# Weighted sums of two attention steps in one burst, with four buffers of exponentials

## The reference

```python
qkv = (x @ Wqkv.T + bqkv).reshape(Bb, Ss, 3, H, HD).transpose(2, 0, 3, 1, 4)
q, k, v = (qkv[0], qkv[1], qkv[2])
attn = jax.nn.softmax(jnp.einsum('bhid,bhjd->bhij', q, k) / jnp.sqrt(jnp.float32(HD)), axis=-1)
...
mod = attn * coh[..., None]
mod = mod / (mod.sum(-1, keepdims=True) + 1e-08)
...
mod = (1.0 - fi) * mod + fi * fa[:, None, :, None]
out = jnp.einsum('bhij,bhjd->bhid', mod, v).transpose(0, 2, 1, 3).reshape(Bb, Ss, Ee)
```

## Time and profile before

| what | value |
|---|---|
| median of 3 runs | 1762.52 us |
| the profiled execution, its time | 1765.92 us |
| its span, first to last instruction | 1764.1 us |
| granted TensorE clock, mean over the span | 0.959 |
| first attention, scores and sums | 116.8 to 485 us |
| TensorE, VectorE, ScalarE busy in 116 to 300 us | 182.03, 155.15, 134.61 us |

### The profile page before, as it was taken

How to read it: one execution, slowest core, us unless ns; L and a number is a source line. 1 busy time by engine, 2 the same in 40 slices (tenths; PEclk the granted TensorE clock), 3 DMA queues, 4 the chain that set the end, 5 groups by cost and what they waited for, 6 DMA issues and landing times. The chain is left out here.

```text
span 1764.1 us, 25261 instructions
## 1 busy us (share of the span) xinstructions
PE 1584.6 (90%) x8692; PEld 1009.6 (57%) x8692; DVE 1159.8 (66%) x1980; ACT 897.0 (51%) x1872; POOL 393.5 (22%) x243
## 2 busy tenths in 40 slices
PE   7789999999968999999978898895999898888698
PEld 3422222222246797878756666663777665665576
DVE  3678888888266464646554953965676873783776
ACT  5137777777813343434325763664434664674442
POOL 3400000000033000000012540553222462262123
PEclk9989999999989999999989999897999999999799
DMA  7621222200003212030033000001002000000010
GB/s 236 125 37 19 37 33 30 30 1 1 1 22 109 72 37 88 19 106 1 0 140 90 1 1 1 0 0 48 1 0 78 1 1 2 0 0 2 23 48 24
DMA packets 59312, 64.74 MB, mean 37 GB/s; under 512 B 15090, under 2 KB 48578, under 8 KB 59220
## 3 DMA queue, kind: packets, MB, share of 16 engines
q1 hardware_dynamic: 57860, 60.24, 13.3%
q10 hardware_dynamic: 1360, 3.41, 0.5%
HBM read 52.95 MB, written 10.49 MB: 36 GB/s over the span
## 5 line engine op out<-in xcount | busy, mean ns | idle before, releaser
L576 DVE TENSOR_REDUCE mcol<-bank 128x1 f32<-128x1024 f32 x256 | 301.4, 1218 | 55.7 <-PE bank L567 55.7
L661 ACT ACTIVATE a_pt<-bank 128x512 f32<-128x512 f32 x512 | 266.3, 602 | 88.4 <-PE bank L693 88.3
L693 PE MATMUL bank<-qa,ka 99*128 99x512 bf16 x512 | 193.0, 384 | 7.2 <-ACT a_pt L661 3.8
L567 PE MATMUL bank<-ka,qa 96*128 96x512 bf16 x512 | 192.7, 386 | 7.4 <-DVE mcol L576 4.2
L1854 PE MATMUL bank<-m_hn,m_w 128*128 128x512 f32 x576 | 151.2, 419 | 18.9 <-DVE m_hn L1985 16.4
L1397 PE MATMUL bank<-wqkv,w_hst 128*128 128x512 f32 x576 | 142.8, 411 | 17.4 <-DVE w_hst L1604 17.4
L1368 POOL TENSOR_TENSOR w_sm<-w_sm,w_st 128x1024 f32<-128x1024 f32 (+1 forms) x64 | 132.3, 2078 | 88.8 <-DVE w_st L1645 88.8
L1854 PEld LDWEIGHTS bank<-m_hn,m_w 128*128 128x128 f32 x576 | 112.2, 195 | 56.2 <-issue 27.3
L693 PEld LDWEIGHTS bank<-qa,ka 99*128 99x128 bf16 x512 | 49.0, 98 | 165.3 <-ACT a_pt L661 120.7
L1443 PE MATMUL bank<-w_kT,w_qz 128*128 128x256 f32 (+1 forms) x512 | 127.3, 385 | 17.9 <-DVE w_st L1638 7.9
L1397 PEld LDWEIGHTS bank<-wqkv,w_hst 128*128 128x128 f32 x576 | 113.2, 197 | 48.1 <-DVE w_hst L1604 20.3
(11 more groups left out here) (237 smaller groups left out, 2673.5 us busy)
## 6 DMA issues: line engine op xcount, KB each, us to landing
f_wex<-in_W SPq DMA_DIRECT2D x8, 2048.0 KB, 11.7
qa<-q_parts SPq DMA_DIRECT2D x48, 128.0 KB, 4.5
ka<-k_parts SPq DMA_DIRECT2D x48, 128.0 KB, 5.3
q_parts<-p_parts SPq DMA_DIRECT2D x16, 192.0 KB, 3.0
k_parts<-p_parts SPq DMA_DIRECT2D x8, 384.0 KB, 3.3
wqkv_raw<-in_wqkv SPq DMA_DIRECT2D x2, 1536.0 KB, 8.8
w<-in_w SPq DMA_DIRECT2D x2, 1536.0 KB, 7.7
phi<-in_phi SPq DMA_DIRECT2D x5, 512.0 KB, 3.7
```

Of the source, the lines that this page charges most:

```text
L567: last = nc.tensor.matmul(max_bank(G, r)[:, jh * HALF:(jh + 1) * HALF], G["qa"][k][0:KS, hg % 2, h, it * P:(it + 1) * P], G["ka"][k][0:KS, ...
L576: nc.vector.reduce_max(G["mcol"][hg % 2][:, p:p + 1], max_bank(G, r)[:, :], X).then_inc(G["max_free"], 1)
L661: nc.scalar.activation(pt[n % 2][:, q, :], sbank(HG * step + q), ACT.Exp, scale=HD0 ** -0.5).then_inc(p_ready, 1)
L693: mm(sbank(i), ka[k][:, q, n * P:(n + 1) * P], qa[k][:, ih, q, :], start=True, stop=True).then_inc(st_ps, 1)
```

## The change

Two things. `pt` has four buffers instead of two, and ScalarE waits for the sums of four steps ago. And `weighted` is called only in even steps, for the two steps before, one right behind the other; in the odd steps none stands, so that the scores and maxima of an odd step and the next even one follow each other without sums between them. The copy of `obank` moves from behind the exponentials of step 0 to behind those of step 1, and the last two steps' sums stand at the end. Banks of scores and of maxima are as before.

```diff
--- before.py
+++ after.py
@@ -623,7 +623,7 @@
         sb = lambda n, s, dt=F32: ctx.enter_context(nc.sbuf_tensor(n, s, dt))
         sem = lambda n: ctx.enter_context(nc.semaphore(n))
         PB, qa, ka, vst, OT = G["PB"], G["qa"], G["ka"], G["vst"], G["OT"]
-        pt = [sb(f"a_pt{s}", [P, HG, HALF]) for s in range(2)]
+        pt = [sb(f"a_pt{s}", [P, HG, HALF]) for s in range(4)]
         st_ps, p_ready, pv_done, o_out = sem("a_st_ps"), sem("a_p_ready"), sem("a_pv_done"), sem("a_o_out")
         sbanks = (PB[0][:, 0:HALF], PB[0][:, HALF:T], PB[1][:, 0:HALF])
         sbank = lambda i: sbanks[i % 3]
@@ -654,13 +654,13 @@
                 for hg in range(HALVES):
                     for n in range(TT):
                         step = TT * hg + n
-                        if step >= 2:
-                            act.wait_ge(pv_done, step - 1)
+                        if step >= 4:
+                            act.wait_ge(pv_done, step - 3)
                         for q in range(HG):
                             act.wait_ge(st_ps, HG * step + q + 1)
-                            nc.scalar.activation(pt[n % 2][:, q, :], sbank(HG * step + q), ACT.Exp,
+                            nc.scalar.activation(pt[n % 4][:, q, :], sbank(HG * step + q), ACT.Exp,
                                                  scale=HD0 ** -0.5).then_inc(p_ready, 1)
-                        if n == 0 and hg >= 1:
+                        if n == 1 and hg >= 1:
                             act.wait_ge(pv_done, TT * hg)
                             nc.scalar.activation(OT[:, (hg - 1) // 2, (hg - 1) % 2 * HALF:((hg - 1) % 2 + 1) * HALF], obank,
                                                  ACT.Copy).then_inc(o_out, 1)
@@ -702,7 +702,7 @@
                     pe.wait_ge(p_ready, HG * (step + 1))
                     for q in range(HG):
                         last = mm(obank[32 * q:32 * q + 32, :], vst[hg // 2 % 2][:, jt, q, :],
-                                  pt[jt % 2][:, q, :], start=(jt == 0), stop=(jt == TT - 1))
+                                  pt[jt % 4][:, q, :], start=(jt == 0), stop=(jt == TT - 1))
                     last.then_inc(pv_done, 1)
 
                 pe.wait_ge(G["ones_in"], GB + 2)
@@ -717,8 +717,10 @@
                                 maxima_to_rows(nc, pe, G, hg + 1)
                             if ahead < HALVES:
                                 score_pair(nc, pe, G, ahead, p0 + q // 2, (q % 2,))
-                        if hg + n > 0:
+                        if n % 2 == 0 and hg + n > 0:
+                            weighted(TT * hg + n - 2)
                             weighted(TT * hg + n - 1)
+                weighted(TT * HALVES - 2)
                 weighted(TT * HALVES - 1)
```

## The result

The changed kernel takes 1788.35 us (median of 4 runs, 1786.33 to 1792.39) against 1762.57 us for the kernel before (1761.11 to 1764.72): a ratio of 1.0148, 95% interval [1.0127, 1.0169]. That is 25.8 us slower, 22 to 30 by the interval. I had predicted 1792 us, 29.1 slower.

What follows compares the result with a forecast made beforehand. The prediction took TensorE to set the pace in the first attention stage, VectorE and ScalarE following with some slack. Terms of 17.6, 8.3, 0.3 and 2.9 us made 29.1, on 1762.5: 1792 us, range 1782 to 1806.

Steps and rivals of the forecast that it cites:

- The burst's saving: Weighted sums of two steps together: the second step costs TensorE 0.86 us instead of 1.09, saving 0.23 us a pair.
- the rival with the dearer step: The second step of a burst costs 1.09 us instead of 0.86: 15 us more, 1806 us; chance 0.08.
- The two banks of maxima: Four pairs of maxima in a row wait 0.39 and 0.26 us for VectorE's reductions: two steps take 6.12 instead of 5.70 us.
- The sign: After the change, TensorE's maxima matmuls (L567) wait for VectorE's reductions (L576) 100 to 115 times, 30 to 40 us in all.
- The cycle with the transpose: Once per half, the maxima are transposed and VectorE starts reducing later: 0.59 us more for that cycle, 14 times.
- The tail: The last 12 steps, without maxima, where scores wait for exponentials: 2.9 us more in all, 1.65 of it from five cycles.
- the copy: ScalarE's copy of the sums (L665) in the tail, between exponentials that scores wait for: about 0.4 us more.
- the 0.86 us for the last sums: At the very end, step 126's sums no longer lie beside step 127's exponentials: one more step of sums, 0.86 us.
- The sum: Ordinary cycles 17.6, those with transposed maxima 8.3, the first cycle 0.3, the tail 2.9: 29.1 us slower.
- a gain: Rival: VectorE frees its banks in time and the waits fall away: 4 us faster, 1758.5 us; chance 0.04.
- The clock: Rival: TensorE's clock falls in the waits, for a tenth of the stage: 20 us more, 1812 us; chance 0.04.

Runs made afterwards that it cites:

- the half exponentials: The changed kernel with each exponential taken of 256 of 512 columns, reductions whole: 1789.29 us in a single run, stage 391.3 us against 396.1.
- the reordering: The changed kernel with the sixteen score and maxima matmuls between two bursts in another order: 1.0107 of the time before, stage 387.2 us.
- before_half_reduce: The kernel before, with VectorE's reductions reading 512 of 1024 columns: 0.9975 of the time before, stage 369.3 us.
- step5_order: The kernel before, with scores moved ahead of maxima in step 5, which holds the transpose: 0.9980 of the time before, stage 365.0 us.
- after_half_reduce: The changed kernel with VectorE's half reductions, reading 512 of 1024 columns: 0.9964 of the time before, stage 366.6 us.
- before_half_both: The kernel before, with reductions reading 512 of 1024 columns and exponentials 256 of 512 (both cuts): 0.9973 of the time before, stage 364.8 us.
- after_half_both: The changed kernel, with reductions reading 512 of 1024 columns and exponentials 256 of 512 (both cuts): 0.9902 of the time before, stage 351.4 us.
- bursts_but_in_tail: The changed kernel, but with single sums from step 5 of half 14 on: 1.0173 of the time before, stage 396.7 us.
- burst_of_four: The changed kernel with sums of four steps together every fourth step and eight exponential buffers: 1.0222 of the time before, stage 405.2 us.

## Why the prediction was right, step by step

- **The burst's saving**, 0.23 us in a pair from the earlier trace rows: 0.24 in an ordinary cycle by the pair of kernels with both cuts. In the changed kernel's trace a double burst takes 1.86 us up to the next score (180.05 to 181.91), as worked out. The cheaper second step of the expert matmuls carried over, and the rival with the dearer step is out.
- **The two banks of maxima**, the step on which all hung: right in place and size. Ordinary cycle 6.11 us (predicted 6.12), 42 of them at 0.42. Read from the starts, the third pair comes 0.47 us late and the fourth 0.17, together 0.64 of the 0.65 predicted. Shown by the half reductions (the loss goes), the half exponentials (it stays), the reordering (it shrinks as priced). The sign "some 100 to 115 times, for 30 to 40 us" came out with 109 times and, by starts, 38 us (27 in the ordinary cycles, 11 in those with the transpose). The profile's own sums are not that number: 68.2 us counts idle weight loads, 16.0 idle matmuls.
- **The cycle with the transpose**: 6.70 us against 6.13 before, 0.57 (predicted 0.59), but for a wrong reason. I wrote that TensorE loses 0.43 us to the transpose in both kernels. The transpose costs 0.12 us of TensorE (182.13 to 182.25 after). In before the other 0.31 is the wait for the reduction of the step before. A second wait, for VectorE's split, lies behind it and costs nothing more: the matmul that it holds starts at 156.70, 0.22 behind its neighbour.

```profile
155.81 0.10 PEld L567 LDWEIGHTS bank<-ka,qa 96*128 96x128 bf16 x1 [0.54 <-DVE mcol L576]
...
156.48 0.38 PE L693 MATMUL bank<-qa,ka 99*128 99x512 bf16 x1
...
156.67 0.10 PEld L567 LDWEIGHTS bank<-ka,qa 96*128 96x128 bf16 x1 [0.31 <-DVE mrow L597]
156.70 0.38 PE L567 MATMUL bank<-ka,qa 96*128 96x512 bf16 x1
```

After, the first is gone (the burst in front gives VectorE time) and the second now costs 0.30, with its matmul at 183.42 instead of 183.12:

```profile
182.13 0.27 PE L582 MATMUL bank<-ident,mcol 128*16 128x128 f32 x1
182.14 0.10 PEld L567 LDWEIGHTS bank<-ka,qa 96*128 96x128 bf16 x1
182.25 0.38 PE L567 MATMUL bank<-ka,qa 96*128 96x512 bf16 x1
...
183.41 0.10 PEld L567 LDWEIGHTS bank<-ka,qa 96*128 96x128 bf16 x1 [0.63 <-DVE mrow L597]
```

  The two kernels lose the same time there only because the split lets TensorE go on 1.50 us behind the step's first score in both, at 156.67 and 183.41. before_half_reduce shows that either wait is enough: without the first, step 5 still takes 3.26 us against 3.28. step5_order confirms it: what is a wait can be filled.
- **The tail**: 2.2 us (it takes 30.53 us after, 28.37 before) where I had 2.9. Five cycles at 0.36 and the copy at 0.36 once more make 2.2, against my 1.65 and 0.4; the term that failed is the 0.86 us for the last sums. Behind the last scores TensorE's order is the same in both kernels, the sums of step 126 and then those of 127, so there was nothing to lose. From the first score of step 127 to the end it takes 3.67 us in both. The sums of step 126 wait only for their own exponentials and lie beside those of step 127; only the second half of the burst waits, 0.99 us. The first row is of before, the next two of after:

```profile
482.88 2.21 PE L704 MATMUL bank<-a_pt,vst 128*32 128x512 f32 x16
```

```profile
509.98 2.21 PE L704 MATMUL bank<-a_pt,vst 128*32 128x512 f32 x16
...
511.12 0.16 PEld L704 LDWEIGHTS bank<-a_pt,vst 128*32 128x32 f32 x8 [0.99 <-ACT a_pt L661]
```

  I had given that burst one wait, for all its exponentials, where it has two, one for each step.
- **The sum**: 17.4 for the ordinary cycles, 8.0 for those with the transpose, 0.3 at the start, 2.2 in the tail: 27.9, and the stage grew by 27.8. Predicted 29.1. The forecast is right because its largest term is; the tail's error of 0.7 and the misread transpose hardly touch the sum.
- **The rivals**: a gain needed shorter reductions. With 0.69 us instead of 1.22 (after_half_reduce) it came, 2.7 us under its base (4 in the prediction); how short they must be was not tried. The clock didn't fall in the cycles' waits of 0.4 us (0.99 and 1.00 in both stretches).

The Trainium skill ("TensorEngine Tiling (Array Packing)", Key Properties) says that a change of tiling mode drains the engine. The traces agree with the 0.24 us saved in an ordinary cycle, in which one burst's entry and exit fall away; that it is a drain which costs this time, no run shows by itself. The same page of the Trainium skill, "PSUM Bottleneck", says that the copying out of PSUM may become the bottleneck. The trace agrees, with the banks of the maxima, which no tiled matmul fills: VectorE's reading of them cost 0.64 us of waits in a cycle, against the 0.24 saved.

## What to carry to other kernels

Before work on the busiest engine is gathered into longer bursts, count how many results the stretch between bursts then hands to each other engine, and compare with the buffers: with two banks the third result waits for the first to be read, however idle the reader is on average. VectorE was busy 84% of the time and had slack in every step; the slack was of use only while the burst came after every second pair. And read the waits of the step that looks dear before giving its price to the instruction in it: here the transpose took 0.12 us and the wait for a bank behind it 0.31.

## What the runs showed of the hardware

- Matmuls on 32-column strips follow each other at an even pace: 16 of them take 1.92 us and 32 take 3.64 (fp32, 512 columns), so that a further step is 0.86 us. Entering and leaving such a burst costs 0.24 us together, by before_half_both (5.69 us for two steps) and after_half_both (5.45).
- In the tail of bursts_but_in_tail a wait of TensorE of 1.6 us was followed by the lower clock level: four score matmuls took 1.97 us from 496.34 on where they take 1.04 at the higher one, and the granted clock of 495 to 500 us was 0.66. The tail of burst_of_four had it too, with waits of 0.2 to 0.6 us and the rows of scores at the exponentials' pace (0.83, 0.66 and 0.83 in the three stretches of 10 us from 490 on). The changed kernel's waits of 0.2 to 0.6 us in every cycle did not bring it (0.99 and 1.00).
- An fp32 transpose of 16 columns of weights by 128 costs TensorE 0.12 us between other matmuls (148.80 to 148.91 in before_half_reduce, 182.13 to 182.25 in the changed kernel), though its record shows 0.27.
